# The gate's first layer on pairs of tiles, and new orders for the stages of the first phase

## What is computed

```python
x = einsum('oc,bchw->bohw', tpl_inv, x);  t = to_tokens(x)
q, k = elu(ln(t) @ Wq.T) + 1, elu(ln(t) @ Wk.T) + 1;  v = ln(t) @ Wv.T     # 8 heads of 16
num, den = causal cumulative sums of q (k v) and q k
t = t + (num / max(den, 1e-6)) @ W_out.T
z = ln(t)
g = (relu(z @ gfc1.T + b) @ gfc2.T + b2).mean(over the 1024 tokens)        # the gate, one row per image
W1m, W2m = W1 + sum_e g_e tv_W1[e], W2 + sum_e g_e tv_W2[e]
t = t + ln(z + relu(z @ W1m.T + b1m) @ W2m.T + b2m) * gain + bias
```

## Time and profile before

| | |
|---|---|
| median of three runs | 749.96 us |
| the profiled execution | 750.53 us, of which the span from first to last instruction is 748.5 us |
| mean granted TensorE clock | 0.979 of full speed |
| first phase, of the span | to 492 us |
| PE, busy over the span | 686.2 us (92%) |
| DVE | 655.6 us (88%) |
| ACT | 648.2 us (87%) |
| POOL | 502.9 us (67%) |

### The profile page before, as it was taken

One profiled execution on the slowest core, in us unless ns is written; L12 is line 12 of the kernel. 1 busy time (PEld: TensorE's weight loads), 2 busy tenths in 40 slices (PEclk: granted clock), 3 DMA queues, 4 the chain that ended last, 5 costly groups with the idle time before them and its releaser, 6 DMA issues. The chain is left out here.

```text
span 748.5 us, 40511 instructions
## 1 busy us (share of the span) xinstructions
PE 686.2 (92%) x13218; PEld 531.7 (71%) x13218; DVE 655.6 (88%) x2487; ACT 648.2 (87%) x1860; POOL 502.9 (67%) x911
## 2 busy tenths in 40 slices
PE   3799899999999999999999999788999998999993
PEld 2567677777777777777777777675777787777772
DVE  5698999999999999999999999747898977998983
ACT  3698999999999999999999999546888876888883
POOL 2678989999999999999999998301333321333333
PEclk9999999999999999999999999989999999999997
DMA  4568766756666766666666656210222111222221
GB/s 140 109 116 135 150 125 140 160 129 138 154 137 135 155 134 136 151 139 142 140 145 141 140 128 123 57 36 2 72 85 82 72 57 30 86 70 84 84 84 70
DMA packets 200294, 82.58 MB, mean 110 GB/s; under 512 B 174028, under 2 KB 187503, under 8 KB 200184
## 3 DMA queue, kind: packets, MB, share of 16 engines
q1 hardware_dynamic: 200248, 81.98, 47.4%
HBM read 22.69 MB, written 17.30 MB: 53 GB/s over the span
## 5 line engine op out<-in xcount | busy, mean ns | idle before, releaser
L878 DVE SCALAR_TENSOR_TENSOR scores_lo<-p_a,scores_hi 128x512 f16<-128x512 f32 x256 | 174.5, 682 | 2.4 <-ACT scores_hi L764 2.2
L764 ACT ACTIVATE scores_hi<-p_a 128x512 f16<-128x512 f32 x256 | 162.4, 643 | 7.0 <-PE p_a L605 6.0
L1411 POOL TENSOR_TENSOR ffn_rstd_shift<-ffn_rstd_shift,consts 128x4 f32<-128x4 f32 x32 | 36.6, 1144 | 113.5 <-DVE ffn_rstd_shift L1369 113.5
L1238 ACT ACTIVATE h_f<-psb,merged_b_of_batch 128x512 f32<-128x512 f32 x128 | 87.3, 712 | 11.7 <-PE psb L1174 10.1
L1347 DVE TENSOR_TENSOR h_lo<-h_f,h_hi 128x512 f16<-128x512 f32 x128 | 95.6, 786 | 1.1 <-ACT h_hi L1249 1.1
L1193 PE MATMUL psb<-merged_W_of_batch,h_hi 128*128 128x128 f16 x512 | 94.3, 220 | 2.2 <-DVE h_lo L1347 1.6
L979 POOL CAST qk_parts<-qk_f 128x512 f16<-128x512 f32 x128 | 78.8, 616 | 24.3 <-issue 20.3
L1194 PE MATMUL psb<-merged_W_of_batch,h_hi 128*128 128x128 f16 x512 | 93.9, 219 | 0.0
L1195 PE MATMUL psb<-merged_W_of_batch,h_lo 128*128 128x128 f16 x512 | 93.8, 219 | 0.0
L622 PE MATMUL p_o<-v_parts,scores_hi 128*128 128x17 f16 x1024 | 90.2, 171 | 2.1 <-issue 0.4
L622 PEld LDWEIGHTS p_o<-v_parts,scores_hi 128*128 128x128 f16 x1024 | 81.2, 96 | 14.3 <-issue 10.8
(11 more groups left out here) (214 smaller groups left out, 2842.4 us busy)
## 6 DMA issues: line engine op xcount, KB each, us to landing
x_f<-in_x SPq DMA_DIRECT2D x32, 256.0 KB, 3.2
t_rows<-t SPq DMA_DIRECT2D x64, 128.0 KB, 2.7
t_back<-t_rows SPq DMA_DIRECT2D x32, 256.0 KB, 2.6
out<-out_tile SPq DMA_DIRECT2D x32, 256.0 KB, 2.0
tv_share<-in_L_ffn_tv_W SPq DMA_DIRECT2D x32, 128.0 KB, 2.2
qkT_parts<-qk_parts SPq DMA_TRANSPOSE x128, 3.1
zT_hi_lo<-z_parts SPq DMA_TRANSPOSE x64, 2.4
merged_W<-in_L_ffn_W SPq DMA_DIRECT2D x2, 256.0 KB, 4.5
```

The costliest lines, as they stand in the source:

```text
L764: nc.scalar.activation(ah[:, t % 2, cols], p_a[:, cols], ACT.Relu).then_inc(ahi_ready[eo], 1)
L878: nc.vector.scalar_tensor_tensor(al[:, t % 2, cols], p_a[:, cols], 0.0, ah[:, t % 2, cols], ALU.max, ALU.subtract).then_inc(alo_ready[eo], 1)
L1238: nc.scalar.activation(hf_[:, c, :], ps[:, c, :], ACT.Relu, bias=b1s[:, h // 2, c:c + 1], scale=1.0 / WS).then_inc(h_ready[c], 1)
```

## The change

Two things change.

First, `gate` and `gate_relu` act at odd tiles only, on two tiles at once. PE's three products have 256 columns instead of 128, and `gate_relu` is one activation over 256 numbers with one sum, into a table of 64 columns instead of 128 (`gate_hidden_sums`). The two reductions that add up the sums of a batch read 4 columns per batch instead of 8. Semaphores count by 2, and `made_by` gives the count on which a stage that shares the bank waits.

```diff
 def gate(b, t):
+    if t % 2 == 0:
+        return
     pe.wait_ge(z_turned[t // 2], 16 * (b + 1))
-    g = p_m2[:, P:2 * P]
-    hi, lo = [x[:, bass.ds(n, 1), :].rearrange("p a c -> p (a c)") for x in (zh, zl)]
+    g = p_m2[:, P:3 * P].rearrange("p (a c) -> p a c", c=P)
+    hi, lo = [x[:, bass.ds(TILES * b + t - 1, 2), :] for x in (zh, zl)]
     mm(g, gfh[:, :], hi, start=True, stop=False)
     mm(g, gfl[:, :], hi, start=False, stop=False)
-    mm(g, gfh[:, :], lo, start=False, stop=True).then_inc(gt_done, 1)
+    mm(g, gfh[:, :], lo, start=False, stop=True).then_inc(gt_done, 2)
...
 def gate_relu(b, t):
+    if t % 2 == 0:
+        return
-    nc.scalar.activation(gjunk[:, :], p_m2[:, P:2 * P], ACT.Relu, bias=gf1b[:, 0:1], scale=1.0 / WS,
-                         accum_out=ghs[:, bass.ds(n, 1)]).then_inc(gate_ready, 1)
+    nc.scalar.activation(gjunk[:, :], p_m2[:, P:3 * P], ACT.Relu, bias=gf1b[:, 0:1], scale=1.0 / WS,
+                         accum_out=ghs[:, bass.ds(TILES // 2 * b + t // 2, 1)])\
+        .then_inc(gate_ready, 2)
...
+def made_by(stage, last, parity):
+    if stage != "gate":
+        return last + 1
+    even = last % 2 == 0 if isinstance(last, int) else parity % 2 == 0
+    return last if even else last + 1
```

```diff
-TENSOR_ORDER = [("gate", 14), ("project", 1), ("state", 3), ("scores", 4), ("conv", 0), ("turn_out", 6),
+TENSOR_ORDER = [("gate", 14), ("project", 1), ("state", 3), ("scores", 4), ("turn_out", 6), ("conv", 0),
                 ("values", 5), ("out_project", 6)]
```

More of the change, by code:

```diff
@@ L39 @@
 BIG = -1.0e30
-TENSOR_ORDER = [("gate", 14), ("project", 1), ("state", 3), ("scores", 4), ("conv", 0), ("turn_out", 6),
+TENSOR_ORDER = [("gate", 14), ("project", 1), ("state", 3), ("scores", 4), ("turn_out", 6), ("conv", 0),
                 ("values", 5), ("out_project", 6)]
[L45 to L53, removed]
+SCALAR_ORDER = [("v_hi", 2), ("normalise", 10), ("split_x", 0), ("tv_hi", 0), ("relu_qk", 2), ("gate_relu", 14),
+                ("read_t1", 7), ("exp_qk", 1), ("state_hi", 3), ("scores_hi_0", 4), ("copy_out", 6),
+                ("scores_hi_1", 4)]
+VECTOR_ORDER = [("invert", 6), ("stats2", 8), ("divide", 6), ("make_qk", 2), ("v_lo", 2), ("mean_var2", 8),
+                ("state_lo", 3), ("stats1", 0), ("tv_lo", 0), ("eps2", 8), ("shift2", 9), ("mean_var1", 0),
+                ("scores_lo_0", 4), ("eps1", 0), ("scores_lo_1", 4)]
+GPSIMD_ORDER = [("split_x", 0), ("rsqrt2", 9), ("qk_hi", 2), ("z_hi", 10), ("qk_lo", 2), ("z_lo", 10),
+                ("rsqrt1", 0)]
+SYNC_ORDER = [("turn_z", 12), ("store", 7), ("turn", 2), ("load_x", 3), ("load_tv", 3)]
 FFN_TENSOR_ORDER = [("up_0", 0), ("up_3", 0), ("up_1", 0), ("down_0", 1), ("down_1", 1), ("down_2", 1),
@@ L152, in build @@
         zh, zl = zz[:, :, 0, :], zz[:, :, 1, :]
[L153 removed]
+        ghs = sb(top, "gate_hidden_sums", [P, NT // 2])
         wm1p = sb(top, "merged_W1", [P, 2, GB * F], F16)
@@ L531, in bank_read @@
                                 for s_ in read:
-                                    at_least(pe, s_, cap(n - before(stage, other) + 1))
+                                    at_least(pe, s_, cap(made_by(other, n - before(stage, other), t)))
                         else:
                             for s_ in uses[previous]:
-                                pe.wait_ge(s_, n - before(stage, previous) + 1)
+                                pe.wait_ge(s_, made_by(previous, n - before(stage, previous), t - before(stage, previous)))
+                    def made_by(stage, last, parity):
[3 more added lines that the diff above has]
+                        return last if even else last + 1
                     def conv(b, t):
@@ L542, in conv @@
                             pe.wait_ge(xl_ready, TILES // 2 * b + t // 2 + 1)
-                        bank_read("conv", n)
+                        bank_read("conv", n, t)
                         o, cols = p_m1[:, 2 * P:3 * P], slice(j * P, (j + 1) * P)
@@ L638, in turn_out @@
                         pe.wait_ge(o_ready, n + 1)
-                        bank_read("turn_out", n)
+                        bank_read("turn_out", n, t)
                         nc.tensor.transpose(p_m2[:, 0:P], o_[:, t % 2, :], ident).then_inc(ot_done, 1)
@@ L644, in out_project @@
                         hf, j = t // HALF, t % HALF
-                        bank_read("out_project", n)
+                        bank_read("out_project", n, t)
                         o, cols = p_m1[:, 0:P], slice(j * P, (j + 1) * P)
```

12 lines of the change are left out of this document (6 added, 6 removed).

## The result

The changed kernel takes 739.51 us, the median of four executions (738.84 to 741.95); the kernel before, with one more execution on that occasion, 750.75 (748.61 to 753.14). The ratio is 0.985, with a 95% interval from 0.983 to 0.988. The forecast was 734 with a range from 722 to 746, so the time lies in the range, 5.5 us above the forecast. Step by step the picture is less kind, as the rest shows: of the 1.20 us per batch that were to be saved, 0.47 came.

What follows compares the result with a forecast made beforehand. ACT's list was taken to set the pace in the steady stretch, with a few tenths of waits per batch. Savings of 12.4 + 3.8 = 16.2 us off 750.5 gave 734 us, range 722 to 746.

Steps and rivals of the forecast that it cites:

- The gate in pairs on ACT: One 256-wide `gate_relu` and one read per pair on ACT: saves 0.23 us per pair, 12.4 us; at the upper bound 4.9.
- `make_qk` ahead of `v_lo`: DVE order: POOL's `qk_hi` can start sooner by `v_lo`, 0.35 us; `exp_qk`'s wait taken as unchanged, could gain 5.3 us.
- `z_lo` ahead of `rsqrt1`: POOL order: `z_lo`, 0.43 us, now precedes `rsqrt1`; `exp_qk` 0.1 us later, taken as unchanged, at worst 1.4 us lost.
- rival 5: The change does nothing, since ACT's fullness could be the effect of others' pace: 750 us; chance 0.07.
- `read_t1` behind the gate: ACT order: two waits behind `normalise` go, 0.28 us per batch, 3.8 us; lower bound 0.
- `stats2` a tile later: On DVE, its wait for `read_t1`, 13.1 us, goes; counted as nothing in time, only as room on DVE.
- The gate in pairs on PE: Three products of 256 columns replace six of 128; counted as nothing because PE does not set the pace.
- Distances on SP: SP's transfers keep a slot or more of distance to their readers, as many issued as before; counted as nothing.
- The second phase: The part of the kernel after the first phase; the prediction took it as not touched by the change.
- Rival 1: Engines' heavy slots do not coincide, each slot lasts as long as its heaviest engine: 27.5 us per batch, 746; chance 0.14.
- Rival 4: Slower: PE's `conv` waits for ACT's later `read_t1` in odd slots; 761 us with 0.5 us per slot; chance 0.08.

## Why the prediction was near, step by step

**The gate in pairs on ACT (12.4 us).** The size was right: 0.37 and 0.10 us per pair, so ACT's list is shorter by about the forecast 0.92 per batch. How much of it reached the time is another matter. The Trainium skill (ScalarE: Activation LUTs, Rules for kernel authors), with about 0.3 us per activation and 0.83 ns per element, would have given 0.51 us for 256 elements as an estimate; the row shows 0.37, so the measured rows were the better guide. But with the pairs alone the batch did not move (27.85 us for 27.80). The step that failed is the sentence "in this stretch the list of ACT sets the pace, with a few tenths per batch for waits". The waits between ACT's starts add up to 1.1 us per batch, of which the prediction named 0.67, and relieved by 0.92 ACT only waited more. Whether ACT's list was one of two limits within 0.1 us of each other (theory L), or only a part of a path that runs over all four engines, the runs do not tell. Fixed distances between most of ACT's starts can't show what comes right behind. By the prediction's own sign (wrong if ACT shows new gaps of more than 0.1 us per slot) the 0.81 us at `gate_relu`, 0.10 per slot, stand just at the bound. The Trainium skill (Perfetto Trace Analysis, Identifying the Most-Contended Engine) advises to optimise the engine with the highest occupancy first; here that was ACT, with 371.4 of 375 us, and relieving it alone gave a ratio of 1.001.

**`make_qk` ahead of `v_lo` (counted as 0 together with `z_lo` ahead of `rsqrt1`, between 5.3 us gained and 1.4 lost).** This is the term that was mis-sized, by the most. Undoing its first half, with `z_lo` left in its new place, costs 0.58 us per batch and 8.6 us in the median. The prediction looked for its effect at `exp_qk`, where ACT waits, and found nothing to gain. The effect is at `qk_hi` on POOL, from 23.7 us of waiting to 7.5, and at `conv` on PE behind it. Without this edit the rest of the change gives nothing, which is the outcome of rival 5. The other half, `z_lo` ahead of `rsqrt1`, counted at up to 0.1 us per batch at `exp_qk`, costs 0.16: so much comes back when it is undone.

**`read_t1` behind the gate (3.8 us).** Its waits behind `normalise` are gone from ACT's timeline, yet no run shows a gain by it: the tables without the pairs bring 0.06 us per batch in all, where this step alone was to bring 0.28. Whether it stands behind the gate or ahead of it makes 0.03 us in the changed kernel. That is near the prediction's lower bound, the wait that turns up again at another instruction. Its old place, ahead of `relu_qk`, was not tried alone.

**`stats2` a tile later (0, room on DVE).** The wait is gone, as said. Undoing it alone was not tried.

**The gate in pairs on PE (0).** Right, for the pair: the tables alone reach the same 27.30 us with eight gates on PE once `gate_relu` is short. But the reason given, that PE does not set the pace, does not hold in the changed kernel: a shorter gate in odd slots does shorten the batch.

**Distances on SP (0, "a slot or more of distance to their readers").** True only with the pairs. With the gate tile by tile, the later `turn_z` costs 50 us.

**The second phase ("not touched").** In code, yes. In the two profiled executions its clock differs, and with it its length, by 5.5 us.

**The rivals.** Rival 1 gave 27.5 us per batch, close to the measured 27.32, and half of its sign is there: POOL runs without idle time through even slots, as from 367.69 to 371.16. But ACT has its gaps in odd slots, at `gate_relu`, and a cut on PE's gate there shortens the batch, so slots as long as their heaviest engine are not what the runs show. That its number came near is luck. Rival 4 was not there: `conv` waits less for `read_t1` than before.

**The number.** That the time came out 5.5 us from the forecast is in part luck: of the forecast 16.2 us twelve steady batches brought 5.7, the term counted at nothing was needed for all of it, and the median before, from which the gain is counted, was a high one. A slip without effect: 0.1 us off each of eight slots leaves 25.5 us of DVE's 26.3, not 25.8.

What stays open: whether ACT's list or a path through several engines held the kernel before; the exact way of the path in the changed kernel; why the medians differ by 9 to 11 us where the steady batches explain 5.7; and which of the other table edits, beside `make_qk`, the gain needs.

## What to carry to other kernels

Before costing what an engine saves, ask how far below it the next limit lies. A busy share of 99% does not make an engine the limit: here its starts still held 1.1 us of waits in a batch of 27.8, and with ACT relieved another path kept the batch within a tenth of a microsecond of it. What counts is found by shortening an instruction, even if part of the work is left out for that, and looking whether the batch follows. And count a swap of two neighbours at nothing only after looking at every engine that waits for either of them.

## What was not expected of the hardware

The granted clock moves one execution by half as much as the change did. The second phase, the same code in every kernel here, took 250.8 to 251.3 us where the clock was at 1.00 on the mean up to its last 30 us, and 256.8 at 0.97 in the kernel before.

In the first phase of the kernel after, the clock fell to a mean of 0.57 from 94 to 102 us, behind 7 us in which the DMA engines were busy throughout (a share of 1.03) and PE waited 0.9 us for transposes of z; PE was busy for 7.63 of the 8 us at the low level. That batch took 3.7 us longer than the one behind it (31.01 for 27.32), but the clock is not all of it. The kernel with one product and a short relu has a clock of 1.00 throughout the same batch, and takes 29.95 us for it, 3.25 above its steady 26.70; the pairs without the tables take 29.35 at 1.00, 1.50 above theirs. What makes the early batches long was not tested, nor whether the wait brought the clock down.
